# Attention beside the next batch's projections: where the queries and keys are turned

## The chip, the cores and the metric

The kernel runs on one core of a Trainium2 chip. The metric is the device time of one execution in microseconds (us), the median of the runs.

## The reference

The input is x of shape (8, 512, 256): 8 batches of 512 tokens. One layer of attention is followed by one of experts; each is added to its input.

```python
x = x + attention(layernorm(x))     # 16 query heads, 4 key/value heads, head size 16,
                                    # rope on q and k, causal softmax, output projection
x = x + experts(layernorm(x))       # 64 experts, the top 8 of each token, and a shared expert

q = rope(x @ Wq.T + bq); k = rope(x @ Wk.T + bk); v = x @ Wv.T + bv
att = softmax(causal(q @ k.T / sqrt(16)))
y = (att @ v) @ Wo.T + bo
```

## The kernel before

The first part of the kernel (about the first 700 us of the profile) is attention, the second part the experts. Only attention is touched.

Five engines run hand-written programs that are kept in step by semaphores. The order of each program comes from one plan, `program`, which calls `beat` once for each batch. A beat has 40 slots, five for each of the 8 pairs of heads. In a beat three batches are worked on at once:

- `main` and `products`: the batch in hand. In each slot PE computes one piece of scores (`pass1`, L511, masked by L518), DVE takes the row maxima of it (L868), and, for an earlier pair, PE computes a transposed piece of scores (`pass2`, L558, masked by L518) and ACT its exponentials (L736). In the third slot of a pair PE turns the maxima (`max_up`, L552) and ACT copies them (L749). In the last two slots of every second pair PE multiplies by the values (`pv`, L607), and ACT copies the result (L763).
- `pre`: the next batch, in four tiles of 128 tokens. Tile t starts in slot 9t and has steps k = 0 to 10, one for each slot. DVE normalizes x (L830), PE turns it in step 2 (L484), ACT copies it (L703), PE projects it to q, k, v in step 3 (L490), DVE adds the bias (L836), DVE and POOL apply rope (L841, L430, L431, L847), ACT rounds q and k in step 7 (L709, L713) and copies v in step 8 (L727), and DVE computes the rounding's remainder in step 8 (L852, L855; semaphore `s_lo`). In step 9 PE turns the queries (8 transposes in two halves, L504) and ACT copies the two halves to `qT` (L721). In step 10 PE turns the keys (8 transposes, L504) and ACT copies two halves to `kT` (L721).
- `post` and `route`: the batch before. Output projection and second normalization (L624 to L648 on PE, L893 to L931 on DVE, L784 to L792 on ACT), and the routing, with 32 scatters on POOL (L463).

The order in a slot is the same on every engine: `route`, `scatter`, `pre` (the later tile first), `main`, `post`, `products`. So the queries are turned and copied at the head of slot 9t + 9 and the keys at the head of slot 9t + 10, before that slot's scores and exponentials. Slots 9 to 10, 18 to 19, 27 to 28 and 36 to 37 are those of tiles 0 to 3.

All these transposes go through the two banks of the PSUM tensor `psp`: half 0 of the queries to bank 0 and half 1 to bank 1, then the keys likewise. The semaphore `s_split` counts ACT's copies, four for each tile: a half of the keys waits for the copy of the same half of the queries (L502), and the next tile's step 2 (slot 9t + 11) writes bank 0 again, once three of the four copies are done (L482); its step 3 waits for the fourth (L488).

Before the first beat a prologue prepares the first batch. It has no other work, its tiles start every 3 slots, and its first three tiles have PSUM banks of their own.

Of the kernel before, what the change touches and what calls it, by code (L numbers as in the profile page):

```python
# [8 lines left out]
F32R = mybir.dt.float32r  # L9
# [7 lines left out]
P = 128  # L17
# [6 lines left out]
TILES = SEQ // P  # L24
# [32 lines left out]
def build(nc, x, const, wqkv, wo, wroute, wgu, wdp, wshd, out):  # L57
# [7 lines left out]
    with ExitStack() as top:  # L65
# [22 lines left out]
        with ExitStack() as ctx:  # L88
# [158 lines left out]
            def beat(steps, h, par, pre=True, main=True, behind=True, late=True):  # L247
                nxt = (h, 1) if par == 0 else (h + 1, 0)
                prv = (h, 0) if par == 1 else (h - 1, 1)
                for slot in range(SLOTS):  # L250
                    p, s = divmod(slot, UNIT)

                    ago = [((h, par, p - n) if main else None) if p >= n else
                           ((*prv, PAIRS_OF_HEADS + p - n) if behind else None) for n in (1, 2)]
                    last_route = 29 if main else 22
                    if behind and not pre and 0 <= slot - last_route < ROUTE_PARTS - 1:
                        steps["route"](*prv, slot - last_route)
                    routed = late and not main
                    if routed and slot == 0:
                        steps["route"](h - 1, par, ROUTE_PARTS - 1)  # L260
                    if late and not routed and 0 <= slot - ROUTE_AT < ROUTE_PARTS:
                        steps["route"](h - 1, par, slot - ROUTE_AT)
                    first, spread = (1, 33) if routed else (SCATTER_AT, SLOTS - SCATTER_AT)
                    for n in range(TILES * TOP):
                        if late and slot == first + n * spread // (TILES * TOP):
                            steps["scatter"](h - 1, par, n)
                    for t in reversed(range(TILES)):
                        k = slot - PRE_AT - PRE_EVERY * t
                        if pre and -PRE_AT <= k < PRE_PARTS:
                            steps["pre"](*nxt, t, k)  # L270
                    steps["main"]((h, par, p) if main else None, *ago, s)
                    for t in reversed(range(TILES)):
                        k = slot - POST_AT - (POST_EVERY * t if pre else (0, 1, 8, 9)[t] if main else t)
                        if behind and -1 <= k < POST_PARTS:
                            steps["post"](*prv, t, k)
                    steps["products"](*ago, s)

            def route_columns(eng, h, par, k):
                b = h * 2 + par
# [49 lines left out]

            def program(eng, steps):  # L330

                for name in ("main", "pre", "post", "route", "scatter", "products"):
                    steps.setdefault(name, lambda *a: None)
                for slot in range(-PRE_AT, FIRST_EVERY * (TILES - 1) + PRE_PARTS):
                    for t in range(TILES):
                        if -PRE_AT <= slot - FIRST_EVERY * t < PRE_PARTS:
                            steps["pre"](0, 0, t, slot - FIRST_EVERY * t)
                half = BATCH // 2
                beat(steps, 0, 0, behind=False, late=False)
                beat(steps, 0, 1, late=False)  # L340
                beat(steps, 1, 0)
                for h in range(1, half - 1):
                    beat(steps, h, 1)
                    beat(steps, h + 1, 0)
                beat(steps, half - 1, 1, pre=False)
                beat(steps, half, 0, pre=False, main=False)
                beat(steps, half, 1, pre=False, main=False, behind=False)
# [123 lines left out]
            def attention_pe(pe):  # L471
# [5 lines left out]
                def pre(h, par, t, k):  # L477
                    tile, u = (h * 2 + par) * TILES + t, t % 2
                    psp, ago = banks(h, par, t)
                    if k == 2:  # L480
                        pe.wait_ge(s_xn, tile + 1)
                        pe.wait_ge(s_split, held(4 * (tile - ago + 1) - 1))  # L482
                        for c in range(KC):
                            last = pe.transpose(psp[:, 0, c * P:(c + 1) * P], xn[u][:, c * P:(c + 1) * P], ident)  # L484
                        last.then_inc(s_xnT_ps, 1)
                    if k == 3:
                        pe.wait_ge(s_xnT, tile + 1)
                        pe.wait_ge(s_split, held(4 * (tile - ago + 1)))  # L488
                        for c in range(KC):
                            last = pe.matmul(psp[:, 1, 0:QKV_D], xnT[u][:, c, :], wqkv_s[:, c, :],  # L490
                                             start=(c == 0), stop=(c == KC - 1))
                        last.then_inc(s_qkv_ps, 1)
                    if k in (9, 10):

                        if k == 9:
                            pe.wait_ge(s_lo, tile + 1)
                            src = qs[u][:].rearrange("p (g a) c d -> p g a c d", a=2)
                        else:
                            src = ks
                        for half in range(2):  # L500
                            if k == 10:
                                pe.wait_ge(s_split, 4 * tile + half + 1)  # L502
                            for n in range(4):
                                last = pe.transpose(psp[:, half, n * P:(n + 1) * P].bitcast(F32R),  # L504
                                                    src[:, 2 * half + n // 2, n % 2].rearrange("p c d -> p (c d)"), ident_r[:])
                            last.then_inc(s_split_ps, 1)

                def scores(h, par, p, bank, at, i, ab):

# [175 lines left out]
                                         start=False, stop=True, skip_group_check=True)  # L685
                        last.then_inc(s_rank_ps, 1)

                program(pe, {"pre": pre, "main": main, "products": products, "post": post, "route": route})

            def attention_act(act):  # L690

# [4 lines left out]
                def pre(h, par, t, k):  # L696
                    b = h * 2 + par
                    tile, u = b * TILES + t, t % 2
                    psp, _ = banks(h, par, t)
                    if k == 2:  # L700
                        act.wait_ge(s_xnT_ps, tile + 1)
                        act.wait_ge(s_qkv_ps, held(tile - 1))
                        act.copy(xnT[u][:], psp[:, 0, 0:D].rearrange("p (k n) -> p k n", k=KC)).then_inc(s_xnT, 1)  # L703
                    if k == 7:

                        act.wait_ge(s_rope, tile + 1)
                        act.wait_ge(s_split_ps, held(4 * tile))
                        flat = rope[u][:].rearrange("p n a d -> p (n a d)")
                        act.copy(qs[u][:, :, 0:2, :], flat[:, 0:D].rearrange("p (n d) -> p n d", d=32).unsqueeze(2)  # L709
                                 .to_broadcast([P, PAIRS_OF_HEADS, 2, 32]))  # L710
                        kh = flat[:, D:QK_D].rearrange("p (g d) -> p g d", d=HEAD_D)
                        for part in (0, 2):
                            last = act.copy(both_places(part), kh.unsqueeze(2).to_broadcast([P, KV_HEADS, 2, HEAD_D]))  # L713
                        last.then_inc(s_hi, 1)
                    if k in (9, 10):
                        if t == 0 and k == 9:
                            act.wait_ge(s_s2, held(40 * (b - 1)))
                        rows = 96 if k == 9 else P
                        for half in range(2):
                            act.wait_ge(s_split_ps, 4 * tile + 2 * (k - 9) + half + 1)  # L720
                            act.copy((qT if k == 9 else kT)[par][0:rows, 4 * half:4 * half + 4, t * P:(t + 1) * P],  # L721
                                     psp[0:rows, half, :].bitcast(F32R).rearrange("p (n c) -> p n c", n=4)
                                     ).then_inc(s_split, 1)
                    if k == 8:
                        act.wait_ge(s_qkv, tile + 1)
                        act.wait_ge(s_pv, held(KV_HEADS * (b - 1)))
                        act.copy(v1[par][:, t, :, 0:HEAD_D],  # L727
                                 qkv[u][:, QK_D:QKV_D].rearrange("p (g d) -> p g d", d=HEAD_D)).then_inc(s_v, 1)

                def exps(h, par, p, s):  # L730
                    b = h * 2 + par
# [68 lines left out]
                        act.wait_ge(s_rank_ps, b + 1)  # L800
                        act.copy(thd[:], psq[:, 384:512].rearrange("p (a e) -> p a e", a=2)).then_inc(s_thd, 1)

                program(act, {"pre": pre, "main": main, "products": products, "post": post, "route": route})

            def attention_dve(dve):

# [750 lines left out]
```

## Time and profile before

| | us |
|---|---|
| median of 3 runs | 1207.75 |
| lowest, highest | 1206.23, 1208.21 |
| the profiled execution, its own time | 1211.74 |
| its span in the profile | 1209.9 |
| PE, DVE, ACT, POOL busy in the span | 1031.7, 705.3, 662.3, 717.5 |

Times in the rows are microseconds from the start of the span. PE is TensorE's matmuls, PEld its weight loads, DVE is VectorE, ACT ScalarE, POOL GpSimd. A PE row's length is modelled, so starts are compared and not ends: the start of one group to the start of the next is what the group costs. `[0.76 <-DVE ks L855]` behind a row is the time that the engine sat idle before it, and the instruction whose end released it. PEclk is the share of full speed that TensorE's clock was granted: 1.00 is 2.4 GHz, 0.50 is 1.2 GHz.

### The profile page before, as it was taken

How to read it: one execution, taken by the hardware profiler on the slowest of the kernel's cores; microseconds unless marked ns; L12 is line 12 of the kernel's file. 1: busy time of each engine (PE TensorE's matmuls, PEld its weight loads, DVE VectorE, ACT ScalarE, POOL GpSimd, SP SyncE). 2: the span in 40 equal slices, each digit the busy share in tenths (PEclk: the TensorE clock that was granted, in tenths of full speed). 3: DMA queues.
4: the chain of work that ended last, by engine and by line, in shares of the span. 5: the costliest groups of instructions: out<-in, count | busy, mean ns of one | idle time of the engine just before them, and what ended most of it. 6: DMA issues, size and time to landing. Idle time of an engine off the chain costs nothing. (4 is left out here: it accounts for less than half of the span.)

```text
span 1209.9 us, 23638 instructions
## 1 busy us (share of the span) xinstructions
PE 1031.7 (85%) x7305; PEld 812.9 (67%) x7305; DVE 705.3 (58%) x2197; ACT 662.3 (55%) x1586; POOL 717.5 (59%) x953
## 2 busy tenths in 40 slices
PE   3699888898989888989998710899989999999985
PEld 1466666666666666656665400899979999989973
DVE  2476676767676767676675370222226666666676
ACT  1466665665565656655654300566656666666651
POOL 3111122774764747747557777377777777777772
PEclk9799999999998999999998855799999999999996
DMA  2388786821321312303222794777769999998755
GB/s 94 130 258 293 237 268 208 278 101 37 108 75 57 111 44 96 114 16 101 79 95 97 275 309 164 214 217 220 219 217 335 343 337 326 366 321 305 250 196 200
DMA packets 142825, 233.20 MB, mean 193 GB/s; under 512 B 17303, under 2 KB 119910, under 8 KB 137840
## 3 DMA queue, kind: packets, MB, share of 16 engines
q1 hardware_dynamic: 67936, 101.06, 25.9%
q0 software_dynamic: 27600, 69.28, 15.9%
q10 hardware_dynamic: 47168, 61.35, 15.4%
q8 instruction: 64, 1.05, 0.4%
q14 instruction: 57, 0.47, 0.1%
HBM read 107.32 MB, written 132.53 MB: 198 GB/s over the span
## 5 line engine op out<-in xcount | busy, mean ns | idle before, releaser
L1495 POOL DMA_INDIRECT res_d<-y,dst_i x319 | 316.7, 993 | 114.6 <-issue 83.4
L463 POOL DMA_INDIRECT rows_d<-pay,slot_i x256 | 256.5, 1002 | 73.4 <-issue 68.4
L868 DVE TENSOR_REDUCE nmax<-ps 128x1 f32<-128x512 f32 (+3 forms) x448 | 225.7, 530 | 103.7 <-PE ps L518 101.4
L736 ACT ACTIVATE wgu_s<-ps 128x512 f32<-128x512 f32 x320 | 191.7, 600 | 95.1 <-PE ps L518 91.5
L1414 PE MATMUL psB<-wgu_s,xT 128*128 x1276 | 172.2, 279 | 4.9 <-ACT innerT L1306 4.1
L518 PE MATMUL ps<-mask,ident_b 128*128 128x256 bf16 (+1 forms) x640 | 173.3, 271 | 0.0
L511 PE MATMUL ps<-kT,qT 96*128 96x512 f32 (+3 forms) x512 | 167.4, 389 | 6.7 <-DVE nmax L868 4.2
L1431 PE MATMUL psD<-wdp_s,innerT 128*128 x638 | 166.9, 385 | 0.0
L558 PE MATMUL ps<-qT,kT 128*128 128x512 f32 (+3 forms) x512 | 162.8, 380 | 0.8 <-ACT qT L749 0.6
L1414 PEld LDWEIGHTS psB<-wgu_s,xT 128*128 128x128 f32 x1276 | 157.9, 195 | 6.1 <-issue 5.8
L1217 DVE TENSOR_TENSOR inner<-inner,psB 128x128 f32<-128x128 f32 x160 | 45.7, 286 | 194.9 <-ACT inner L1302 189.8
L1402 PE MATMUL psA<-cst,xg 128*128 128x128 f32 x638 | 98.2, 277 | 51.9 <-DMA xg<-rows_d 51.9
L1313 ACT COPY y<-psD 128x512 f32<-128x512 f32 x160 | 93.7, 586 | 78.6 <-PE psB L1422 64.6
L1297 ACT COPY xT<-psA 128x512 f32<-128x512 f32 x160 | 93.0, 581 | 55.0 <-PE psA L1402 55.0
L1431 PEld LDWEIGHTS psD<-wdp_s,innerT 128*128 128x128 f32 x638 | 110.0, 193 | 9.0 <-issue 0.6
L1402 PEld LDWEIGHTS psA<-cst,xg 128*128 128x128 f32 x638 | 76.9, 144 | 53.1 <-DMA xg<-rows_d 52.8
L511 PEld LDWEIGHTS ps<-kT,qT 96*128 96x128 f32 x512 | 88.7, 202 | 31.5 <-DVE nmax L868 15.4
L518 PEld LDWEIGHTS ps<-mask,ident_b 128*128 128x128 bf16 x640 | 63.7, 100 | 64.1 <-issue 36.3
L1244 DVE SCALAR_TENSOR_TENSOR acc<-yk,rw_all,acc 128x256 f32<-128x256 f32 x202 | 97.5, 483 | 4.5 <-DMA yk<-res_d 0.3
L558 PEld LDWEIGHTS ps<-qT,kT 128*128 128x128 f32 x512 | 89.6, 202 | 3.3 <-ACT wgu_s L736 1.5
L1302 ACT ACTIVATE inner<-psB 128x128 f32<-128x128 f32 x160 | 44.4, 278 | 72.6 <-PE psA L1402 72.6
L607 PE MATMUL psv<-wgu_s 128*32 128x512 f32 (+3 forms) x1024 | 82.8, 442 | 0.7 <-ACT wgu_s L736 0.7
(264 smaller groups left out, 1579.5 us busy)
## 6 DMA issues: line engine op xcount, KB each, us to landing
rows_d<-blank ACTq DMA_DIRECT2D x8, 5440.0 KB, 19.5
xg<-rows_d SPq DMA_DIRECT2D x160, 272.0 KB
yk<-res_d SPq DMA_DIRECT2D x28, 1024.0 KB
wgu_s<-wgu_in ACTq DMA_DIRECT2D x8, 1024.0 KB, 14.4
x_d<-x SPq DMA_DIRECT2D x30, 192.5 KB, 2.7
xs<-x_d SPq DMA_DIRECT2D x30, 192.5 KB, 2.8
res_d<-y,dst_i POOLq DMA_INDIRECT x319
wgu_s<-x_in SPq DMA_DIRECT2D x32, 128.0 KB, 2.1
```

The costliest lines, as they stand in the source:

```text
L463: pool.indirect_dma_start(rows_d, bass.IndirectOffsetOnAxis(ap=slot_i[par][:, t, k:k + 1], axis=0), pay[par][:, t, :], None).then_inc(s_sc ...
L511: pe.matmul(ps1[:, bank, at:at + keys], qT[par][0:96, p, i * P:(i + 1) * P], kT[par][0:96, 2 * (p // 2) + ab, 0:keys], start=(at == 0), st ...
L518: return pe.matmul(blocks, ident_b[:], mask[:].unsqueeze(1).to_broadcast([P, blocks.shape[1], P]), start=False, stop=True, skip_group_chec ...
L558: pe.matmul(ps2[:, bank, at:at + n], kT[par][:, 2 * (p // 2) + ab, kt * P:(kt + 1) * P], qT[par][:, p, kt * P:SEQ], start=(at == 0), stop= ...
L736: act.activation(pexp[p % 4][:, s, :], ps2[:, (5 * p + s) % 2, :], ACT.Exp, scale=HEAD_D ** -0.5).then_inc(s_exp, 1)
L868: return dve.tensor_reduce(nmax[u][:, tile, heads[0]:heads[-1] + 1], src, AX.X, ALU.max, negate=True)
L1244: dve.scalar_tensor_tensor(out=acc[:, u], in0=yk_at(tile)[:, k], scalar=rw_all[:, at:at + 1], in1=xs_at(tile)[:, 0:D] if k == 0 else acc[: ...
L1313: act.copy(y[:, 2 * i % Y:2 * i % Y + 2, :].rearrange("p b h -> p (b h)"), psD[:, i % 2, :]).then_inc(e_d, 1)
L1402: last = pe.transpose(psA[:, i % 2, (b * KC + c) * P:(b * KC + c + 1) * P], xg[:, (2 * i + b) % G, c * P:(c + 1) * P], ident)
L1414: last = pe.matmul(psB[:, i % B, b * GU:(b + 1) * GU], xT[:, i % A, b, c, :], wgu_s[:, bass.ds(off + c * GU, GU)], start=(c == 0), stop=(c ...
L1431: last = pe.matmul(psD[:, i % 2, b * D:(b + 1) * D], innerT[:, i % A, b, :], wdp_s[:, bass.ds(off, D)], start=True, stop=True)
L1495: pool.indirect_dma_start(res_d, bass.IndirectOffsetOnAxis(ap=dst_i[:, j % (2 * G):j % (2 * G) + 1], axis=0), y[:, j % Y, :], None, bounds ...
```

## The change

Step 9 of `pre` becomes empty. The queries are turned by PE, and copied by ACT, at the head of slot 9t + 10, where the keys were. A new step `keys` is called at the end of the same slot, after `products`: PE turns the keys there, ACT copies them there. The numbers of instructions, the semaphores and what they are waited for at stay as they are. The prologue calls `keys` right behind step 10.

```diff
                     steps["products"](*ago, s)
+                    for t in reversed(range(TILES)):
+                        k = slot - PRE_AT - PRE_EVERY * t
+                        if pre and k == PRE_PARTS - 1:
+                            steps["keys"](*nxt, t)
...
                             steps["pre"](0, 0, t, slot - FIRST_EVERY * t)
+                            if slot - FIRST_EVERY * t == PRE_PARTS - 1:
+                                steps["keys"](0, 0, t)
...
-                    if k in (9, 10):
-
-                        if k == 9:
-                            pe.wait_ge(s_lo, tile + 1)
-                            src = qs[u][:].rearrange("p (g a) c d -> p g a c d", a=2)
-                        else:
-                            src = ks
+                    if k == 10:
+                        pe.wait_ge(s_lo, tile + 1)
+                        src = qs[u][:].rearrange("p (g a) c d -> p g a c d", a=2)
                         for half in range(2):
-                            if k == 10:
-                                pe.wait_ge(s_split, 4 * tile + half + 1)
-                            for n in range(4):
-                                last = pe.transpose(psp[:, half, n * P:(n + 1) * P].bitcast(F32R),
-                                                    src[:, 2 * half + n // 2, n % 2].rearrange("p c d -> p (c d)"), ident_r[:])
-                            last.then_inc(s_split_ps, 1)
+                            turn_parts(psp, half, src)
+
+                def keys(h, par, t):
+                    tile = (h * 2 + par) * TILES + t
+                    psp, _ = banks(h, par, t)
+                    for half in range(2):
+                        pe.wait_ge(s_split, 4 * tile + half + 1)
+                        turn_parts(psp, half, ks)
+
+                def turn_parts(psp, half, src):
+
+                    for n in range(4):
+                        last = pe.transpose(psp[:, half, n * P:(n + 1) * P].bitcast(F32R),
+                                            src[:, 2 * half + n // 2, n % 2].rearrange("p c d -> p (c d)"), ident_r[:])
+                    last.then_inc(s_split_ps, 1)
...
-                    if k in (9, 10):
-                        if t == 0 and k == 9:
+                    if k == 10:
+                        if t == 0:
                             act.wait_ge(s_s2, held(40 * (b - 1)))
-                        rows = 96 if k == 9 else P
                         for half in range(2):
-                            act.wait_ge(s_split_ps, 4 * tile + 2 * (k - 9) + half + 1)
-                            act.copy((qT if k == 9 else kT)[par][0:rows, 4 * half:4 * half + 4, t * P:(t + 1) * P],
-                                     psp[0:rows, half, :].bitcast(F32R).rearrange("p (n c) -> p n c", n=4)
+                            act.wait_ge(s_split_ps, 4 * tile + half + 1)
+                            act.copy(qT[par][0:96, 4 * half:4 * half + 4, t * P:(t + 1) * P],
+                                     psp[0:96, half, :].bitcast(F32R).rearrange("p (n c) -> p n c", n=4)
                                      ).then_inc(s_split, 1)
...
+                def keys(h, par, t):
+                    tile = (h * 2 + par) * TILES + t
+                    psp, _ = banks(h, par, t)
+                    for half in range(2):
+                        act.wait_ge(s_split_ps, 4 * tile + half + 3)
+                        act.copy(kT[par][:, 4 * half:4 * half + 4, t * P:(t + 1) * P],
+                                 psp[:, half, :].bitcast(F32R).rearrange("p (n c) -> p n c", n=4)
+                                 ).then_inc(s_split, 1)
```

## Rows read from the trace of the kernel before

**Rows 1.** The page, the span in 40 equal slices: PE and its clock.

```profile
PE   3699888898989888989998710899989999999985
PEclk9799999999998999999998855799999999999996
```

**Rows 2.** Waits of PE from 45 to 600 us: total, times, longest.

```profile
PE psp L504 <- DVE ks L855: 19.0, 15, 2.2
PE psp L504 <- ACT qT L721: 9.3, 7, 1.5
...
PE psp L484 <- DVE wgu_s L830: 4.2, 8, 0.7
```

**Rows 3.** Busy time by window, a whole beat: PE, PEld, DVE, ACT, POOL, PEclk, DMA.

```profile
284.40:366.00 81.60, 73.22 (x540) 52.34 (x536) 56.55 (x169) 48.34 (x106) 50.89 (x79) 0.94 0.23 78
```

**Rows 4.** Timeline, slots 9 to 11: tile 0. Start, length, engine, line.

```profile
287.58 0.24 ACT L727 COPY wgu_s<-wgu_s 128x64 f32<-128x64 f32 x1 [5.18 <-PE psv L607]
...
288.36 1.07 ACT L721 CAST qT<-psp 96x512 fp32r<-96x512 f32 x2
...
289.00 1.02 PE L504 MATMUL psp<-ident_r,ks 128*128 128x128 f32 x8 [1.55 <-ACT qT L721]
289.31 0.62 ACT L736 ACTIVATE wgu_s<-ps 128x512 f32<-128x512 f32 x1
...
289.80 1.09 ACT L721 CAST kT<-psp 128x512 fp32r<-128x512 f32 x2
...
290.69 0.44 PE L484 MATMUL psp<-cst,wgu_s 128*128 128x128 f32 x2
290.75 0.63 ACT L763 COPY oT<-psv 128x512 f32<-128x512 f32 x1
```

**Rows 5.** Timeline, slot 19: tile 1, PE and ACT.

```profile
307.14 0.88 PE L504 MATMUL psp<-ident_r,ks 128*128 128x128 f32 x8
307.85 0.47 PE L511 MATMUL ps<-kT,qT 96*128 96x256 f32 x2
...
307.71 1.07 ACT L721 CAST kT<-psp 128x512 fp32r<-128x512 f32 x2 [0.81 <-PE psp L504]
```

**Rows 6.** Timeline, slots 27 to 29: tile 2.

```profile
322.27 0.68 DVE L868 TENSOR_REDUCE nmax<-ps 128x1 f32<-128x512 f32 x1
322.41 0.88 PE L504 MATMUL psp<-ident_r,qs 128*128 128x128 f32 x8 [0.76 <-DVE ks L855]
...
323.48 0.54 PE L552 MATMUL ps<-ident_r,mt 128*128 128x128 f32 x4
...
327.81 0.44 PE L484 MATMUL psp<-cst,wgu_s 128*128 128x128 f32 x2
```

**Rows 7.** Timeline, slots 36 and 37: tile 3, then the same of two beats earlier.

```profile
338.86 0.28 PE L518 MATMUL ps<-mask,ident_b 128*128 128x256 bf16 x1
...
340.97 0.87 PE L504 MATMUL psp<-ident_r,qs 128*128 128x128 f32 x8 [1.83 <-DVE ks L855]
...
341.91 0.57 POOL L447 TENSOR_TENSOR rstd<-rstd,minus_half 128x1 f32<-128x1 f32 x1
...
342.87 0.41 DVE L918 TENSOR_SCALAR pay<-x,mv,rstd 128x256 f32<-128x256 f32 x1
...
345.55 0.74 PE L511 MATMUL ps<-kT,qT 96*128 96x384 f32 x2
...
180.23 0.88 PE L504 MATMUL psp<-ident_r,qs 128*128 128x128 f32 x8 [1.68 <-DVE ks L855]
...
183.81 0.50 PE L511 MATMUL ps<-kT,qT 96*128 96x384 f32 x2
```

**Rows 8.** Windows of 2 us, columns as in rows 3: behind tile 3's stop.

```profile
344.00:346.00 2.00, 2.00 (x12) 1.91 (x12) 0.75 (x2) 1.26 (x4) 1.63 (x2) 0.50 0.37 139
```

**Rows 9.** Timeline of the prologue, PE.

```profile
26.46 1.25 PE L504 MATMUL psp<-ident_r,qs 128*128 128x128 f32 x8 [0.17 <-DVE ks L855]
27.51 2.89 PE L490 MATMUL ps<-wgu_s 128*128 128x384 f32 x4
```

More of the change, by code:

```diff
@@ L330, in program @@
             def program(eng, steps):
-                for name in ("main", "pre", "post", "route", "scatter", "products"):
+                for name in ("main", "pre", "keys", "post", "route", "scatter", "products"):
                     steps.setdefault(name, lambda *a: None)
@@ L686, in route @@
                         last.then_inc(s_rank_ps, 1)
-                program(pe, {"pre": pre, "main": main, "products": products, "post": post, "route": route})
+                program(pe, {"pre": pre, "keys": keys, "main": main, "products": products, "post": post, "route": route})
             def attention_act(act):
@@ L801, in route @@
                         act.copy(thd[:], psq[:, 384:512].rearrange("p (a e) -> p a e", a=2)).then_inc(s_thd, 1)
-                program(act, {"pre": pre, "main": main, "products": products, "post": post, "route": route})
+                program(act, {"pre": pre, "keys": keys, "main": main, "products": products, "post": post, "route": route})
             def attention_dve(dve):
```

## The prediction

> **What bounds the kernel now.** The page's slices come first: PE is busy at 80 to 90% through attention, with the clock mostly near full [rows 1]. A whole beat by windows shows 73.22 us of PE in 81.60, against 56.55 of DVE, 50.89 of POOL and 48.34 of ACT [rows 3]. So PE sets the pace, and only its stops can be won. The list of its waits then says which: the transposes of queries and keys (L504) stop it for 19.0 us on DVE's remainder and 9.3 us on ACT's copy of the queries, the largest two in the list [rows 2]. The timeline of a beat then shows which tile stops, and what is late behind each. In a steady beat tile 0 waits 1.55 us at the keys [rows 4], tile 1 not at all [rows 5], tile 2 0.76 us at the queries [rows 6], tile 3 1.83 us at the queries [rows 7]: 4.14 us. Six of the seven beats that prepare a batch look like this (batches 1 to 6); the first has no batch behind it.
>
> **The prices that recur.** Eight transposes hold PE for 307.85 - 307.14 = 0.71 us [rows 5]. ACT starts on half 0 of them 307.71 - 307.14 = 0.57 us after their start [rows 5]. Two copies of a half take 1.07 us together; a lone one is put at 0.58, since the second starts 0.49 behind the first, so 0.49 is the step from one to the next (289.31 to 289.80 has the same step behind an exponential) [rows 4]. PE starts 0.06 us after the copy it waits for (288.36 + 0.58 = 288.94, PE at 289.00) [rows 4]. No instruction is added or removed: PE's busy time stays, and the sum is one of stops.
>
> **The new stop, for tiles 0, 1 and 2.** The next tile's transposes of x (L484) open slot 9t + 11 and need the copy of the keys' half 0. Before, these transposes came a whole slot after the keys. Now the keys are the last thing of slot 9t + 10 and L484 is the next instruction. From the keys' start PE would reach it at 0.71, but the copy ends at 0.57 + 0.58 and PE sees it at 1.21: a stop of 0.50 us if ACT is free. Queued behind L484 on PE is everything, scores first. ACT is free in slot 19 and 28, where value products stand between the last scores and the keys and the exponential runs under them. If ACT were still in the exponential, add its step of 0.49, so 0.50 to 1.0; I take 0.50, since these slots have the products.
>
> **Tile 1.** Nothing is removed (no wait before): +0.50 us.
>
> **Tile 2.** Without the queries PE gets through slot 27's scores during the old wait, but then stands at `max_up` (L552), which needs slot 26's maxima: these come right behind the remainder on DVE, at 322.27 + 0.68 = 322.95, so L552 starts at 323.01, not 323.48 [rows 6]. That is 0.47 earlier, but with 0.71 us of queries still to do: +0.24. The stop of 0.76 has gone to another wait on DVE. Then the key copy's 0.50, of which I take off 0.20: the value products of slot 28 leave PE free at about 327.6 and L484 began at 327.81 [rows 6], the x it needs being late anyway. Together +0.54 us. Ends: -0.76 (the stop gone whole, the new one covered) and +1.24.
>
> **Tile 3.** PE ran out of work about 339.15 and began the queries at 340.97 [rows 7]. Now it does slot 36's scores first, 0.71 us (two pieces with masks), and waits from 339.85: a stop of 1.1 in place of 1.83. Behind the remainder DVE must do two maxima and then `pay` (L918), for which POOL's L447 ends at 341.91 + 0.57 = 342.48; so `pay` ends at 342.94 (0.41 long, start to start about the same as now) [rows 7]. PE reaches L643, which needs it, at 342.52 and stops again, to 343.0. Then 0.19 for L643, 0.36 for the scores, 0.71 for the keys: slot 38 starts at 344.26. Before, at full clock, slot 38 began 183.81 - 180.23 = 3.58 us after the queries [rows 7], which is 344.55. So -0.29 us. No tile follows here, so the keys' copies are late for nobody before slot 40. Ends: -1.83 and 0.
>
> **Tile 0.** PE waited because ACT was late: ACT stood 5.18 us for slot 9's value products before it copied v [rows 4], a step-8 copy with slot 8's exponential behind it. That wait stays. Without the queries in slot 9 it ends 0.71 earlier, at 286.87. ACT then has to do: v's copy 0.15, exponential 0.49, a routing copy 0.14, exponential 0.49, two query copies 0.98, the copy of the output 0.50, exponential 0.49, and 0.58 for the keys' half 0. L484 follows at 290.75, where it was at 290.69 [rows 4]. The stop of 1.55 is exchanged for two or three shorter ones of the same sum. The output's copy is earlier than its 290.75 and may give back 0.1. I take 0. Ends: -1.55 (ACT does not bind) and +0.3.
>
> **First beat and prologue.** In the first beat three stops of 0.50 are added and about half of what tiles 2 and 3 wait there (1.32 in all, by the same list) goes: +0.8. In the prologue the third tile's projection waited behind the first tile's queries, 27.51 - 26.46 = 1.05 us later at half clock [rows 9]. Now it goes first, and the queries use the time in which DVE handles it; the keys wait a copy of 0.58 instead. I take -0.8, between 0 and -1.6 (two such places).
>
> **Sum.** 6 x (0 + 0.50 + 0.54 - 0.29) = 4.5; + 0.8 - 0.8 = +4.5 us. SP's loads, POOL's scatters and the experts hang on PE's progress and shift with it. The profiled execution took 1211.74 us, 1.84 over its span and 4.0 over the median. 1211.74 + 4.5 = 1216.2 on its own scale; on that of the median 1207.75 + 4.5 = 1212.2.
>
> The Trainium skill says (Perfetto Trace Analysis, Optimizing Tensor Performance, Matmuls) that independent groups on PE should rotate through different PSUM banks, so that one group is taken out under the next group's matmuls. It speaks against this change, which puts queries, keys and the next x into the same two banks with less between them. Were the banks rotated, the key-copy stops of tiles 1 and 2 would go and the sum would be some 5 us lower; no run here shows that yet.
>
> **Rivals.** (A) DVE does not come next: the queries' stops of tiles 2 and 3 go whole, 0.76 + 1.83 a beat, 15.5 us in six, and the key-copy stops cost 12 x 0.50 = 6. With the prologue's 0.8 this is -10: 1197.5. For it: DVE has 25 us of slack in a beat [rows 3]. Against it: its next results after the remainder, maxima and `pay`, are due at once. (B) The clock decides, faster. In the beat at 340.97 the clock fell to 1.2 GHz behind tile 3's stop [rows 8], and slot 38 came 345.55 - 340.97 = 4.58 us after the queries where the beat without a fall took 3.58 [rows 7]: 1.0 us a fall. By windows of 2 us like that of rows 8 the clock fell 11 times from 120 to 600 us, behind tile 3's stop in five of six steady beats and behind tile 0's 1.55 in three. If only such long unbroken stops cause it, eight falls go: 4.5 - 8 = -3.5, so 1204. For it: the new stops are 0.5 to 1.2 long. Against it: their sum near each place is unchanged. (C) It cancels: a few falls go, or the stops of 0.50 are covered by waits that PE has next in any case: 1208, no change. (D) The clock falls more: at tile 2 a wait of 0.8 at L629 and one of 1.2 at L552 would stand close together. One more fall a beat is +6: 1218. The rival of the other sign is B; it decides from five falls fewer on.
>
> The Trainium skill (Perfetto Trace Analysis, Optimization Strategy) tells one to find the gaps on the most contended engine, see what blocks, and make that come sooner. The change does that for L504, and by that rule alone the time would be A's; the rows of tiles 2 and 3 show the next blocker behind each gap.
>
> **How the numbers follow.** Forecast 0.40, A 0.12, B 0.15, C 0.20, D 0.13. The predicted time is 1212. The unknown costs taken from both sides move it by 0.5 x 12 us upwards (ACT busy at the keys) and by a similar sum downwards; with B and D this gives 1203 to 1219, which leaves A out. About 0.2% (2.4 us) is what a measurement can tell from no change. Faster: A and B, 0.27. Same: C, 0.20. Slower: forecast and D, 0.53.
>
> **What would show it.** After the change L504 should wait for DVE only for tile 3, near 1.1 us, and L484 should wait for ACT's kT copy (L721's successor) near 0.5 us at tiles 1 and 2 and over 1 us at tile 0. L552 should wait about 0.9 to 1.2 us for DVE in slot 27, and L643 half a microsecond in slot 37. A beat at full clock should be 0.7 us longer. I am wrong if L484 does not wait, if L552's wait stays under 0.5, or if the count of stretches at 0.50 of the clock (11 from 120 to 600 us) changes by five or more.

## The result, and the profile after

The changed kernel took 1215.27 us (median of 4 runs, 1211.2 to 1217.22) beside 1206.99 for the kernel before: ratio 1.0066, 95% interval 1.0036 to 1.0096. A second measurement with 12 runs gave 1212.21 us and 1.0035, interval 1.0013 to 1.0056. It is slower by 4 to 8 us by the two ratios. The profiled execution took 1211.2 us with a span of 1209.4, the fastest of the four and no slower than the 1211.74 of the kernel before: single executions scatter by more than the change is worth.

The page's slices stand against [rows 1]:

```profile
PE   3699898888988889889998620899999999999985
...
PEclk9699999999998999998998855799999999999997
```

In PE's row no slice differs by more than one tenth, and of the clock's slices three differ by one tenth (the second and the nineteenth lower, the last higher): the page doesn't tell the two kernels apart. PE's waits from 45 to 600 us do (engine, line, what it waited for: total, times, longest), against [rows 2]:

```profile
PE psp L490 <- ACT kT L745: 12.6, 21, 1.0
PE ps L563 <- DVE nmax L887: 12.5, 22, 1.3
PE psp L515 <- DVE ks L874: 8.1, 7, 2.3
PE psq L654 <- DVE pay L937: 7.8, 6, 1.3
PE ps L522 <- DVE nmax L887: 6.1, 14, 0.8
...
PE psp L515 <- ACT qT L731: 2.6, 7, 0.4
```

L515 is the old L504 (queries and keys), L490 the old L484 (the next x), L563 the old L552 (`max_up`), L522 the scores (old L511), L654 the old L643. The wait for the remainder has fallen from 19.0 to 8.1 us and that for the queries' copy from 9.3 to 2.6. In their place stand 12.6 us at L490, which waited for no copy of keys before, and more at L563 and L522, which wait for maxima. All waits of this list come to 59.1 us, of before's to 54.4.

A beat without a fall of the clock, against [rows 3] (window; length; busy PE, PEld, DVE, ACT, POOL; PEclk; DMA share; GB/s):

```profile
271.87:351.22 79.35, 70.08 (x537) 49.35 (x537) 57.96 (x168) 48.27 (x107) 50.76 (x81) 1.00 0.24 81
```

The stops of this beat, by PE's timeline (start, length, line, what; in brackets the idle time before it and its releaser), against [rows 4 to 7]:

```profile
287.98 1.02 PE L515 MATMUL psp<-ident_r,ks 128*128 128x128 f32 x8 [0.45 <-ACT qT L731]
290.02 0.41 PE L490 MATMUL psp<-cst,wgu_s 128*128 128x128 f32 x2 [1.01 <-ACT kT L745]
...
308.59 0.41 PE L490 MATMUL psp<-cst,wgu_s 128*128 128x128 f32 x2 [0.42 <-ACT kT L745]
...
321.32 0.50 PE L563 MATMUL ps<-ident_r,mt 128*128 128x128 f32 x4 [1.09 <-DVE nmax L887]
...
326.72 0.41 PE L490 MATMUL psp<-cst,wgu_s 128*128 128x128 f32 x2 [0.43 <-ACT kT L745]
...
338.07 0.50 PE L522 MATMUL ps<-kT,qT 96*128 96x512 f32 x1 [0.82 <-DVE nmax L887]
...
340.76 0.88 PE L515 MATMUL psp<-ident_r,qs 128*128 128x128 f32 x8 [0.97 <-DVE ks L874]
342.39 0.40 PE L654 MATMUL psq<-cst,pay 128*128 128x128 f32 x2
```

The whole case stands here. Tile 0's 1.55 has become 0.45 + 1.01. Tile 1 has a new 0.42. Tile 2's 0.76 has become 1.09 + 0.43. Tile 3's 1.83 has become 0.97. L654 does not wait behind it, though the sum had a stop of 0.48 there. And a stop of 0.82 that no step of the sum had stands 2.7 us ahead of it.

So that stops can be read apart from the clock, attention is cut at the first transposes of x of each tile, and only stretches at full clock are compared. The first column of a kernel is from x of tile 0 to x of tile 1, and so on; "falls" counts the stretches at 0.50 of the clock from 70 to 600 us (by windows of 2 us, as in [rows 8]) in the profiled execution.

| kernel | ratio to before | tile 0 | tile 1 | tile 2 | tile 3 | beat at full clock | falls |
|---|---|---|---|---|---|---|---|
| before | 1 | 18.00 | 18.18 | 17.47 | 24.32* | 77.97 | 11 |
| changed | 1.0066, 1.0035 | 18.15 | 18.57 | 18.13 | 24.49 | 79.34 | 7, 8 |
| e2 keys late only | 1.0095 | 18.8 | 20.2** | 17.9 | 24.32 | - | 10 |
| e3 both at the head | 1.0081 | 17.75 | 18.65 | 18.39 | 25.12 | 79.94 | 6 |
| e4 keys between | 0.9997 | 17.42 | 18.59 | 18.03 | 25.24 | 79.28 | 2 |
| e5 x behind scores | 0.9939 | 18.01 | 18.24 | 17.78 | 24.17 | 78.20 | 1 |
| e6 remainder later | 0.9925 | 18.15 | 18.57 | 17.60 | 23.50 | 77.83 | 6 |
| e8 e5 and e6 | 0.9924 | 18.02 | 18.23 | 17.24 | 24.8 | 78.27 | 3 |
| e9 xb early | 0.9952 | 18.16 | 18.55 | 18.12 | 23.44 | 78.27 | 4 |
| e7, e10 by tile | 0.988, 0.9859 | 17.43 | 18.32 | 17.48 | 24.04 | 77.27 | 4, 4 |
| e11 by tile, xb early | 0.9898 | 17.44 | 18.31 | 17.45 | 24.04 | 77.24 | 5 |

\* Before has no tile 3 stretch without a fall in a steady beat (25.6 and more with one). The 24.32 is the only one of e2, whose tile 3 has its queries where before has them, so before's beat of 77.97 and what is reckoned from it are estimates. In beat 1, which is shorter, before took 24.59 without a fall and the changed kernel 23.42. ** All with a fall. The beats of before and e10 are the sum of their columns. The four of e9 include the end of a long stretch that began at 60.5. In e5 and e8 x itself stands later in its slot, behind the turning of the maxima too at tile 0, which makes their tile 3 column longer and their tile 0 column shorter than by the others' cut; their beat compares.

At full clock a steady beat is 1.37 us longer than before (79.34 against 77.97). A fall costs 1.47 by tile 1 of before (19.65 with and 18.18 without); by the other columns it is 1.2 to 1.6. Beat by beat, from the first mark of attention (51.62 and 51.65 us) to the last (570.41 and 574.61); "lost" is one minus the granted clock, summed over windows of 2 us, and one fall is 1.7 of it:

| | first beat | 1 | 2 | 3 | 4 | 5 | 6, to the last mark |
|---|---|---|---|---|---|---|---|
| before, us | 62.79 | 77.40 | 80.90 | 80.70 | 82.28 | 79.62 | 55.10 |
| lost | 5.58 | 1.70 | 3.44 | 3.40 | 5.14 | 1.70 | 1.70 |
| changed, us | 64.40 | 76.48 | 79.34 | 79.35 | 83.09 | 80.77 | 59.53 |
| lost | 5.68 | 0.00 | 0.00 | 0.00 | 5.10 | 1.72 | 5.12 |

The changed kernel is 4.2 us later at the last mark (4.97 in the second profiled execution). It has five falls fewer in beats 1 to 3 and two more in beat 6: net three, some 4.4 us at 1.47 each. So its stops cost 4.2 + 4.4 = 8.6 us to this point, of which 1.6 in the first beat. Time won with the clock hides half of the time lost to stops.

What comes behind the last mark (mostly the experts) scatters by as much as the change is worth: 639.5 us in the kernel before, 634.8 and 639.3 in the two profiled executions of the changed kernel. That is why the total of a single profiled execution doesn't show the 4.2 us.

### The profile page after: what moved, and what is told of

It reads as the page before. It is cut to its first block and busy times, and to the rows that moved or that the text cites. A ratio compares the mean times of both kernels' runs of the same rounds, so it can differ in the third digit from the quotient of the medians.

```text
span 1209.4 us, 23638 instructions
## 1 busy us (share of the span) xinstructions
PE 1025.9 (85%) x7305; PEld 806.2 (67%) x7305; DVE 706.0 (58%) x2197; ACT 662.1 (55%) x1586; POOL 716.5 (59%) x953
## 3 DMA queue, kind: packets, MB, share of 16 engines
q8 instruction: 64, 1.05, 0.4%
## 5 line engine op out<-in xcount | busy, mean ns | idle before, releaser
L522 PE MATMUL ps<-kT,qT 96*128 96x512 f32 (+3 forms) x512 | 166.3, 387 | 9.7 <-DVE nmax L887 7.4
L522 PEld LDWEIGHTS ps<-kT,qT 96*128 96x128 f32 x512 | 87.7, 200 | 40.4 <-DVE nmax L887 24.0
```

Of the source, the lines that this page charges most:

```text
L522: pe.matmul(ps1[:, bank, at:at + keys], qT[par][0:96, p, i * P:(i + 1) * P], kT[par][0:96, 2 * (p // 2) + ab, 0:keys], start=(at == 0), st ...
```

## Experiments

**e1: the changed kernel again,** without an edit.

> The changed kernel once more, for the size and the scatter of its time. Theory S (stops): at equal granted clock it is 4 to 5 us over the kernel before, as the stops add up (0.75 us in each of six beats), and what is measured beyond that goes with a lower mean clock of the run. Theory N (next waits): the stops themselves cost 8 us or more, and the difference at equal clock is 8. In its trace the transposes of x wait about 0.43 us for the keys' copy at tiles 1 and 2 and 1.0 at tile 0.

Measured: 1212.21 us, ratio 1.0035 (1.0013 to 1.0056), 12 runs; the same list of waits, near 60 us in all. The sign holds; the middles of the two measurements are 4 and 8 us, their intervals together 1.6 to 11.6. Of the two theories N is nearer: the stops cost some 8 us to the last mark (7.7 to 8.6, below), and the mean clock of the timed runs is not lower than before's (0.933 for 0.931).

**e2: only the keys late.** The queries go back to slot 9t + 9, on PE and ACT:

```diff
-                    if k == 10:
+                    if k == 9:
```

> One part of the change alone: the keys are turned and copied at the end of slot 9t + 10, the queries stay at the head of slot 9t + 9. If the new stop of the x transposes behind the keys' copies is what costs, this is the worst of all: all stops of before stay (0.76, 1.83 at tiles 2 and 3) and the x transposes wait 0.4 to 0.5 us at tiles 1 and 2 and about 0.7 us more than now at tile 0: 1.6 us a beat, 9 to 11 us slower than before. If the queries' move is what costs, it is within 2 us of before.

Measured: 1221.26 us, ratio 1.0095 (1.0067 to 1.0123), 11.5 us slower by the ratio where 9 to 11 was expected. The keys' copy stops the next x as often as in the changed kernel (21 times) but for longer, and the remainder's wait stays near that of before:

```profile
PE psp L515 <- DVE ks L874: 18.4, 15, 2.3
PE psp L490 <- ACT kT L745: 15.6, 21, 1.5
```

So moving the keys costs, and moving the queries as well wins 3 to 7 us of it back. That does not make the queries' move a gain by itself, as e3 shows.

**e3: both at the head of slot 9t + 10.**

```diff
                         if pre and -PRE_AT <= k < PRE_PARTS:
                             steps["pre"](*nxt, t, k)
+                        if pre and k == PRE_PARTS - 1:
+                            steps["keys"](*nxt, t)
...
-                        if pre and k == PRE_PARTS - 1:
-                            steps["keys"](*nxt, t)
```

> The other part alone: queries a slot later, and the keys right behind them at the head of slot 9t + 10 (before that slot's scores). The x transposes should not wait for the keys' copies any more, but the keys wait 0.5 us for the copy of the queries at tiles 1 to 3 and about 1.3 us at tile 0. By stops: tile 0 -0.3, tile 1 +0.5, tile 2 +0.74, tile 3 -0.4, so +0.5 us a beat: 2 to 4 us slower than before, near the changed kernel. If only the keys' place costs, it is faster than before by the queries' stops of 2.6 us a beat (up to 15 us).

Measured: 1218.27 us, ratio 1.0081 (1.0053 to 1.011): three times what was expected. Waits at full size:

```profile
PE psp L513 <- ACT qT L729: 16.0, 29, 1.2
PE ps L561 <- DVE nmax L885: 12.9, 22, 1.3
```

Queries and keys share two PSUM banks. Back to back, the keys wait for the queries' copies at every tile (29 times). The scores between the two in the changed kernel are what hides most of that copy (2.6 us of waits for 16.0). So each half of the change alone costs more than both together, 11.5 and 9.8 us by the ratios for 4 to 8: the two depend on each other.

**e4: keys between scores and the post stage** (the same call, placed right behind `steps["main"]`; no other edit).

> The keys are turned and copied in the middle of slot 9t + 10, behind the slot's first scores and ahead of post and products; queries at its head as in the change. By stops both new waits shrink: the keys wait 0.15 us for the queries' copy at tile 1, the x transposes find the keys copied. Tile 0 -0.7, tile 1 +0.15, tile 2 +0.4 (its wait for DVE's maxima stays near 1.1), tile 3 -0.75: -0.9 us a beat, with the prologue 5 to 8 us faster than before, 10 to 13 faster than the changed kernel. If the stops are not what sets the time, it is within 2 us of the changed kernel.

Measured: 1208.35 us, ratio 0.9997 (0.9974 to 1.002): no change against before, where 5 to 8 us were expected. Its beat at full clock, 79.28, is that of the changed kernel (79.34); what it has over that kernel stands beside two falls of the clock for seven and eight. Tile 0 gained 0.73 a beat. Tile 1 gained nothing, and tile 3 got longer (25.24). ACT now copies keys ahead of the transposed x2, and PE waits for that instead:

```profile
PE psp L515 <- ACT qT L731: 5.4, 8, 0.9
...
PE psq L659 <- ACT x2T L806: 2.4, 6, 0.4
```

**e5: x's transposes behind the scores of slot 9t + 11,** on PE and on ACT, so that something stands between keys and x:

```diff
                     steps["main"]((h, par, p) if main else None, *ago, s)
+                    for t in reversed(range(TILES)):
+                        if pre and slot - PRE_AT - PRE_EVERY * t == 2:
+                            steps["turn_x"](*nxt, t)
```

`turn_x` holds what step 2 of `pre` did.

> The changed kernel, with the next tile's transposes of x, and ACT's copy of them, one place later in their slot: behind that slot's first scores. If the changed kernel loses by these transposes waiting for the keys' copies, the 0.35 us of scores now runs in that wait: at tiles 1 and 2 it falls from 0.43 to 0.1, at tile 0 from 1.0 to about 0.65. That is 1 us a beat: 5 to 7 us faster than the changed kernel, so within 2 us of the kernel before. If the waits only stand for a lag of another engine, the time stays with the changed kernel and the wait turns up elsewhere.

Measured: 1201.9 us, ratio 0.9939 (0.9915 to 0.9962), faster than before and than expected. The key-copy stop is mostly gone, and more stands at `max_up`:

```profile
PE ps L571 <- DVE nmax L898: 18.2, 28, 1.3
...
PE psp L517 <- ACT kT L749: 4.1, 7, 0.6
```

**e6: tile 2's remainder behind the maxima of its slot** on DVE:

```diff
-                    if k == 8:
+                    if k == 8 and not (t == 2 and tile >= TILES):
+                        remainder(tile, u)
...
+                def late_rest(h, par, t):
+                    if t == 2:
+                        remainder((h * 2 + par) * TILES + t, t % 2)
```

`late_rest` is called behind `steps["main"]`.

> The changed kernel, with DVE's step 8 of tile 2 (the rounding's remainder) behind that slot's maxima instead of ahead of them. The prediction's step is that tile 2's old stop went to the turning of the maxima in slot 27, because the remainder (0.7 us) stands ahead of them on DVE. Then that wait falls from 1.09 us to about 0.4 in each of six beats, and the stretch from tile 2's x to tile 3's shrinks from 18.1 to 17.4: 3 to 4 us faster than the changed kernel. If DVE is behind for other reasons, the wait stays above 0.9.

Measured: 1202.51 us, ratio 0.9925 (0.9901 to 0.9949). The stop of 1.09 in slot 27 is 0.55 here:

```profile
400.63 0.51 PE L566 MATMUL ps<-ident_r,mt 128*128 128x128 f32 x4 [0.55 <-DVE nmax L896]
```

By the ratios that is 13 to 17 us under the changed kernel, where 3 to 4 were expected. The edit gives 0.53 a beat in tile 2's column. But tile 3's column, which the edit does not touch, fell by 0.99: there is no stop of 0.82 ahead of tile 3's queries in this kernel. That led to e9.

**e7 and e10: an order chosen tile by tile.** Tile 0 has its queries a slot later and its keys behind the scores, tiles 1 and 2 are as before, tile 3 is as changed:

```diff
-                    if k == 10:
+                    if k == (10 if t in (0, 3) else 9):
```

with `keys` called at the head of the slot for tiles 1 and 2, behind `main` for tile 0 and at the end for tile 3.

> The place that was best for each tile: tile 0 queries a slot later and keys behind the first scores (as in the run with the keys between), tiles 1 and 2 as in the kernel before, tile 3 as in the changed kernel. From the beats measured so far the stretches are 17.4 (tile 0; before 18.0), 18.2, 17.5 and 24.5 (tile 3; before about 24.8 at full clock, 25.6 to 26 with the fall of the clock that mostly followed its stop). By stops alone 0.9 us a beat less than before: 5 us faster than the kernel before. If the falls behind the stops of 1.83 and 1.55 us go too, up to 8 us more. If waits just move (as between the changed kernel and the one with the keys between), no faster than before.

> The order chosen tile by tile once more (tile 0's queries a slot later with its keys behind the scores, tiles 1 and 2 as before, tile 3 as the change has it): ratio to the kernel before 0.985 to 0.991 if the first measurement stands, 0.994 or above if half of it was a chance of the clock in that batch.

Measured: e7 1193.56 us, ratio 0.988 (0.9851 to 0.991); e10 1193.11 us, ratio 0.9859 (0.984 to 0.9878). It beats both kernels, 14 to 17 us under the one before, more than the 5 to 13 expected of e7; e10 repeats it. No wait for copies of keys is left at x's transposes (e10):

```profile
PE psp L519 <- DVE ks L878: 13.9, 14, 2.2
PE psq L658 <- DVE pay L941: 8.6, 10, 1.3
PE ps L567 <- DVE nmax L891: 5.4, 15, 0.5
PE psp L519 <- ACT qT L735: 5.1, 7, 0.9
PE psp L494 <- DVE wgu_s L853: 4.7, 11, 0.7
```

At full clock it gains 0.70 a beat, and the mark at the end of attention stands at 555.26 us, 15.2 ahead of before. Stops explain some 5.5 us of that (six beats, 1.3 in the first); most of the rest goes with the clock: four falls to this mark instead of ten. Why its tile 3, ordered as in the changed kernel and without e9's collision, takes 24.04 and not the 23.44 of e9 stays open.

**e8: e5 and e6 together.**

> The last two edits together on the changed kernel: x turned behind the scores, and tile 2's remainder behind the maxima. If both waits are real costs they add: 8 to 11 us faster than the changed kernel, 2 to 6 faster than the kernel before. If they stand for one lag, the two together bring no more than the larger.

Measured: 1200.7 us, ratio 0.9924 (0.9901 to 0.9947): no more than either alone, as the expectation's second case has it. Tiles 1 and 2 got both gains (18.23, 17.24), but tile 3 took 24.8 where e5, cut at the same places, has 24.17: its queries wait 1.22 for the remainder (e5: 0.95) and PE then 0.22 for `pay`. Gains at different places of a beat did not add here, since the beat's later part moved against DVE and POOL.

**e9: POOL's residual sum a slot early** (L447, `xb`), ahead of two scatters:

```diff
-                    if k == 1 and not ending(h, par):
+                    if k == 0 and not ending(h, par):
```

> The changed kernel with POOL's residual sum (xb, L447) one slot earlier, ahead of the two scatters instead of behind them; nothing else moves. In the changed kernel's beat from 271.87 us, DVE's L950 took 0.76 (0.22 elsewhere) and the L866 behind it 1.01 (0.48), while POOL ran a scatter (335.25 to 336.21) and then L447 (336.24 to 337.00); the maxima behind them came late and PE stopped 0.82 at L522. Theory (DVE operations with two inputs in SBUF and POOL's operations that read SBUF hold each other up): L866 has no instance above 0.55 in slot 36 of tile 3's stretch, the 0.82 stop shrinks below 0.2, tile 3's stretch falls from 24.49 to 23.6 to 23.9 us, and five such beats give 3 to 4.5 us against the changed kernel (its ratio to the kernel before 1.0035 to 1.0066, so 1.000 to 1.003 here). The lengthening of L950 stays if the scatter causes it and goes if L447 does. Rival (the long durations are an artefact of the records, the stop comes from the order of DVE's work alone): the stop at L522 stays at 0.6 or more and the time is that of the changed kernel.

Measured: 1204.6 us, ratio 0.9952 (0.9936 to 0.9967), 8 to 11 us under the changed kernel by the medians and 10 to 14 by the ratios, where 3 to 4.5 was expected. First the place in the changed kernel, DVE and POOL:

```profile
335.25 0.96 POOL L469 DMA_INDIRECT rows_d<-pay,slot_i  x1 [0.30 <-issue]
336.24 0.76 POOL L447 TENSOR_TENSOR xb<-xr,cst 128x256 f32<-128x256 f32 x1
...
335.66 0.76 DVE L950 TENSOR_TENSOR chosen<-left,logit 128x64 bf16<-128x64 f32 x1
336.34 1.01 DVE L866 TENSOR_TENSOR wgu_s<-wgu_s 128x320 f32<-128x320 f32 x1
337.27 1.34 DVE L887 TENSOR_REDUCE nmax<-ps 128x1 f32<-128x384 f32 x3
```

Then the same place in e9:

```profile
335.32 0.75 POOL L447 TENSOR_TENSOR xb<-xr,cst 128x256 f32<-128x256 f32 x1
336.23 1.25 POOL L469 DMA_INDIRECT rows_d<-pay,slot_i  x1 [0.17 <-issue]
...
335.99 0.23 DVE L950 TENSOR_TENSOR chosen<-left,logit 128x64 bf16<-128x64 f32 x1
336.13 0.48 DVE L866 TENSOR_TENSOR wgu_s<-wgu_s 128x320 f32<-128x320 f32 x1
336.53 1.35 DVE L887 TENSOR_REDUCE nmax<-ps 128x1 f32<-128x384 f32 x3
...
337.39 0.47 PE L522 MATMUL ps<-kT,qT 96*128 96x512 f32 x1
```

DVE's two operations take 0.23 and 0.48 again, the maxima are back in time, and L522 has no stop. A beat with the collision is 1.08 longer than one without (79.35 and 78.27, by tile 3's column alone: 24.49 and 23.44). The expectation counted five such beats. The trace of the changed kernel has three, beats 2, 3 and 5, with an L866 of 1.01, 1.01 and 1.00; beats 4 and 6 have a fall of the clock at tile 2, just ahead, and no collision, and beat 1 has none either (its tile 3 took 23.42). The second profiled execution agrees: falls at tile 2 and no collision in beats 2 and 4, collisions in 3, 5 and 6. So the collisions are worth 3.2 us. What is over that goes with the clock: four falls for seven or eight. The mean granted clock over all timed runs is 0.940 for e9, 0.930 and 0.933 for the two measurements of the changed kernel.

**e11: the order by tile with `xb` early.**

> The same with L447's sum a slot earlier. The order by tile shows no lengthened L866 (mean 484 ns), so the theory of the two engines holding each other up has nothing large to take away: within 0.3% of e10, with L853 (475 ns mean against 411 before) back at 411 to 475. The rival that POOL's order matters for the post stage whatever DVE meets gives over 3 us to either side.

Measured: 1197.18 us, ratio 0.9898 (0.9882 to 0.9914), 0.4% slower than e10 and outside what was expected, with five falls for four and 0.8 more in the first beat; its beat at full clock (77.24) is that of e10. Moving `xb` is no gain in itself. It helps where it ends a collision.

## Why the prediction was right, and where it was not

The forecast was 1212 us, 4.5 over the kernel before, and the two measurements are 1215.3 and 1212.2, 8.3 and 4.3 over it. The sign, its mechanism (stops exchanged, not won) and the range hold. That the total is so close is partly luck: the stops cost nearly twice what was forecast, and falls of the clock that the sum left out gave about half of it back.

**Tile 1: right.** Forecast +0.50 a beat, measured +0.39; the new stop at L490 is 0.42. e5 takes it away and the column returns to 18.24.

**Tile 2: right.** Forecast +0.54, measured +0.66. `max_up` waits 1.09, where 0.9 to 1.2 was written, behind DVE's remainder; e6 proves the cause. The 0.20 taken off for cover was not there: the key-copy stop is 0.43 here as at tile 1.

**Tile 0: right on the whole.** Forecast 0, measured +0.15, as 0.45 + 1.01 in place of 1.55. ACT's order counts, as was said: e4, in which the keys are turned and copied ahead of ACT's copy of the output, wins 0.73. (e4 moves them on PE too, so that ACT alone sets the place is argued and not shown.)

**Tile 3: two steps failed, in opposite directions.** The queries wait 0.97 (1.1 forecast). The second stop, 0.48 at L643's successor for `pay`, never came: POOL's L453 ran at 340.68 instead of the 341.91 that the sum took over from before [rows 7], and `pay` was ready. In the kernel before POOL was in a scatter from 340.46 to 341.54 when DVE's result for it came; in the changed kernel it had waited 0.90 for that result. Without the collision the column is 23.44 against 24.32: -0.88, not -0.29. The sum had kept POOL where it stood while it moved PE and DVE. The same omission, with the other sign, missed the collision of L866 with POOL's `xb`, +1.05 in the beats that have it. Net +0.17 there.

**First beat and prologue: wrong in size.** The first beat grew by 1.6, not 0.8. The prologue's third projection did start earlier, at 26.60 instead of 27.51 [rows 9], but further on the queries wait for DVE's remainder in both kernels, until 41.49 before and 41.54 now, and the first mark stands at 51.65 (before 51.62): 0, not -0.8. Before and after:

```profile
41.49 0.87 PE L504 MATMUL ps<-ident_r,qs 128*128 128x128 f32 x8 [2.31 <-DVE ks L855]
...
26.60 2.93 PE L496 MATMUL ps<-wgu_s 128*128 128x384 f32 x4 [0.46 <-ACT wgu_s L714]
...
41.54 0.87 PE L515 MATMUL ps<-ident_r,qs 128*128 128x128 f32 x8 [2.26 <-DVE ks L874]
```

**The sum.** Stops cost 8.6 us to the last mark where 4.5 was forecast. Of the 4.1 missing, three collisions are 3.2, first beat and prologue 1.6, tiles 0 to 2 together 0.16 a beat or 1.0; tile 3's better relief takes 0.59 back in five beats, 3.0. That is 2.8. The last 1.3 is mostly the price of a fall. Column against column the ten falls of before come to 14.3 us and the seven of the changed kernel to 10.8, an estimate (it rests on the 24.32 of e2) by which the difference is 3.5 and not 4.4, and the stops cost 7.7. Beat 1 has another 0.4: its tile 2 took 17.90 for 16.86, 1.04 more and not 0.66. On the other side stand three falls fewer, 3.5 to 4.4 us in the profiled execution, which the forecast put at nothing.

**Rival B (the clock)** was half true: falls went from 11 to 7 and 8, short of the five fewer from which it decides, and each is worth 1.2 to 1.6 and not 1.0. How much of that holds on average stays open: over all timed runs the mean clock is 0.930 and 0.933 for the changed kernel and 0.930 to 0.931 for the one before, a smaller gain than the profiled executions show. The falls changed place too. Before's eleven stood behind tile 3's queries (five), tile 0's keys (three) and a stop of 1.32 for `pay` (two), and one behind no stop over 0.5. The changed kernel's seven stand at or behind tile 0's new stop of 1.01 (three), the stop for `pay` (two) and the pair of stops at tile 2 (two), and none behind tile 3's 0.97.

**Rival D (the clock falls more)** came in two of six beats at the place that it named. At tile 2 stops of 0.78 (L640) and 1.08 (L563) stand close together, and the clock fell behind them at 404.3 and 568.2 us, where the kernel before had no fall in any beat; the second profiled execution has two as well.

```profile
403.85 0.51 PE L563 MATMUL ps<-ident_r,mt 128*128 128x128 f32 x4 [1.08 <-DVE nmax L887]
...
404.00:406.00 2.00, 2.00 (x9) 1.65 (x9) 0.85 (x4) 0.58 (x1) 1.70 (x2) 0.58 0.32 120
```

These falls were outweighed by the five that went at tile 3. Rival A is refuted by 1.09 at L563: DVE did come next. Rival C (no change) is outside both intervals, though the lower ends, 1.0013 and 1.0036, come near it.

The Trainium skill's rule on rotating PSUM banks (Perfetto Trace Analysis, Optimizing Tensor Performance, Matmuls) was put at some 5 us. e5 did not rotate banks, but put work between two uses of the same one: L490's wait fell from 12.6 to 4.1 us, and the kernel was some 1% faster than the changed one, though with one fall of the clock for seven or eight. A rotation itself was not tried.

## What to carry to other kernels

When a step moves on one engine, redraw the other engines' order around it: a stop is set by the latest of them, and those that look idle enough (POOL here) decide by where they stand, not by how busy they are. A delay that suits one tile of a loop can hurt the next; choosing the place tile by tile won 1.2 to 1.4% where the uniform rule lost 0.3 to 0.7%. Compare stretches at equal clock before crediting or blaming an edit, and count the clock's falls apart.

## What the runs showed of the hardware

**DVE and POOL can hold each other up.** In the changed kernel L866 took (count; min, median and max in ns):

```profile
L866 DVE TENSOR_TENSOR wgu_s<-wgu_s x32: 471/484/1011, 18.9 to 583.8; 128x320 f32<-128x320 f32 x32
```

and in e9, the same line with only POOL's order changed:

```profile
L866 DVE TENSOR_TENSOR wgu_s<-wgu_s x32: 473/484/493, 19.2 to 575.5; 128x320 f32<-128x320 f32 x32
```

The long instances began while POOL was in a sum that reads SBUF and ended 0.35 us after it (336.24 + 0.76 = 337.00, and 337.35). The Trainium skill (SBUF — State Buffer, Who interferes with whom) says that a VectorE instruction with two inputs in SBUF and a GpSimd instruction that reads SBUF exclude each other, the first to issue holding the other off. L866 agrees with that. What held L950 (0.76 for 0.22) was by the traces the sum and not the scatter. Beside a scatter alone that operation kept 0.22 to 0.28 in every kernel, as in the kernel before:

```profile
239.95 0.96 POOL L463 DMA_INDIRECT rows_d<-pay,slot_i  x1 [0.30 <-issue]
240.58 0.23 DVE L931 TENSOR_TENSOR chosen<-left,logit 128x64 bf16<-128x64 f32 x1
```

In e11, where the scatter had ended, it took 0.80 beside the sum alone:

```profile
330.32 0.74 POOL L451 TENSOR_TENSOR xb<-xr,cst 128x256 f32<-128x256 f32 x1
330.34 0.80 DVE L954 TENSOR_TENSOR chosen<-left,logit 128x64 bf16<-128x64 f32 x1
```

How the sum can hold L950 in the changed kernel, where its record begins 0.58 behind L950's start (336.24 and 335.66), is not shown. That DVE also holds POOL's scatters is suggested only: in e9 one that began behind L866 took 1.25 in place of 0.96. The same lengthening stood in the trace of the kernel before, at another operation with two inputs, while POOL ran its own part of rope (11 of 32 took over 0.75):

```profile
L841 DVE TENSOR_TENSOR wgu_s<-wgu_s,cst x32: 479/482/1069, 16.5 to 575.5; 128x320 f32<-128x320 f32 x32
```

The collision is in e3 and e4 too (longest L866 or its counterpart 1015 and 1014 ns) and in none of before, e2 and e5 to e11 (none over 500). All kernels with it are no faster than before, though e2, which is the slowest, is without it.

**The clock's falls stand behind single stops, but not behind all of them, and not in proportion to waiting.** The kernels faster than before all ran at a mean clock of 0.938 to 0.943 over their timed runs, those that were not at 0.930 to 0.937, while the total of PE's waits differs little (before 54.4 us, e6 52.0, e5 54.0). (This mean is over the whole execution; in the profiled ones 47 to 58 us of clock are lost behind the last mark of attention and 15 to 32 ahead of it.) In the kernel before ten of the eleven falls came directly behind a stop of 1.3 to 1.8 us (the one of 1.83 ended at 340.97, the fall began at 342.7), and seven such stops had no fall behind them. In the changed kernel beats 2 and 3 had no fall and beat 6 three, with the same stops. Splitting long stops seems to avoid some falls; which of them bring one was not settled.
